# A four-layer decoder in one kernel: a scaled and shifted norm moved into the linear attention's pipeline, with four smaller rearrangements

## The reference

```python
def _L1_attn_ref(x, Wq, bq, Wk, bk, Wv, bv, Wc, We, Wo, bo, gamma, beta):
    residual = x
    ...
    num = einsum('bhsf,bhsfd->bhsd', qf, kv_cum)
    den = einsum('bhsf,bhsf->bhs', qf, cumsum(kf, axis=2))[..., None] + EPS
    o = num / den ...
    y = residual + (o @ Wo + bo)
    return (y - mean(y)) / sqrt(var(y) + LN_EPS) * gamma + beta
# caller: x = x + _L1_attn_ref(_layernorm(x), ...)
# _L1_xattn_ref: "focus" attention on the first 16 tokens of each sequence of x and of ctx
# _L2_attn_ref: Mamba forward and backward; per state s of 16:
#   h = dA_t * h + dBx_t;  y += h * C_t;   dBx = dt * x * B_t
#   then gelu(fwd + bwd + h), a norm, an FFN with gelu
```

## Time and profile before

| | |
|---|---|
| Median of 3 runs | 7387.59 us (7383.5 to 7392.11) |
| The profiled execution | 7383.77 us, span 7382.0 us |
| Busy in the span | PE 6509.4 (88%), DVE 5385.0 (73%), ACT 4114.1 (56%), POOL 2863.0 (39%) |
| Granted TensorE clock, mean | 0.955 of full speed |
| DMA | 190.34 MB, mean 26 GB/s |

### The profile page before, as it was taken

How to read it: one execution, slowest core, us unless ns; L and a number is a source line. 1 busy time by engine, 2 the same in 40 slices (tenths; PEclk the granted TensorE clock), 3 DMA queues, 4 the chain that set the end, 5 groups by cost and what they waited for, 6 DMA issues and landing times. The chain is left out here.

```text
span 7382.0 us, 189639 instructions
## 1 busy us (share of the span) xinstructions
PE 6509.4 (88%) x74836; PEld 3954.8 (54%) x74836; DVE 5385.0 (73%) x8866; ACT 4114.1 (56%) x6062; POOL 2863.0 (39%) x1653
## 2 busy tenths in 40 slices
PE   7989994887697898888998969989899999989998
PEld 5767672443442333333333346667576766667676
DVE  7867476665556999999999955678577777768544
ACT  3556343665446777777766765556344444456433
POOL 3311184332215888888877701156022222211000
PEclk9999997999898999999999989989999999999999
DMA  1000001000001222222212100000000000000000
GB/s 28 0 21 12 2 0 19 3 3 2 15 1 55 74 74 74 74 80 73 73 69 72 58 11 15 10 31 3 12 2 2 2 2 2 2 15 14 2 0 23
DMA packets 115919, 190.34 MB, mean 26 GB/s; under 512 B 38661, under 2 KB 74747, under 8 KB 114971
## 3 DMA queue, kind: packets, MB, share of 16 engines
q1 hardware_dynamic: 115482, 184.01, 7.8%
HBM read 173.87 MB, written 7.98 MB: 25 GB/s over the span
## 5 line engine op out<-in xcount | busy, mean ns | idle before, releaser
L2589 POOL TENSOR_TENSOR m_dBx<-m_dtx,m_Bs 128x1024 f32<-128x1024 f32 x515 | 1205.4, 2357 | 227.6 <-DVE m_hs L2955 185.9
L2955 DVE TENSOR_TENSOR_SCAN m_hs<-m_ps_dA,m_dBx 128x512 f32<-128x512 f32 x1030 | 1199.7, 1204 | 72.5 <-POOL m_dBx L2589 58.2
L2707 PE MATMUL m_ps_y<-m_yc,ident 128*128 128x512 f32 x2060 | 1054.7, 636 | 0.0
L2811 ACT ACTIVATE m_ps_dA<-m_dt,m_A 128x504 f32<-128x504 f32 x1030 | 683.2, 678 | 486.7 <-DVE m_hs L2955 483.9
L2086 POOL TENSOR_TENSOR a_s<-a_s,a_den 128x1024 f32<-128x1024 f32 x128 | 243.7, 1904 | 1125.1 <-DVE a_den L2132 1125.1
L2966 DVE TENSOR_TENSOR m_yc<-m_hs,m_ps_C 128x1024 f32<-128x1024 f32 x515 | 615.0, 1194 | 6.3 <-PE m_ps_C L2688 5.4
L2707 PEld LDWEIGHTS m_ps_y<-m_yc,ident 128*128 128x128 f32 x2060 | 358.7, 194 | 370.4 <-issue 370.4
L2688 PE MATMUL m_ps_C<-m_parts,m_sel 48*128 48x512 bf16 x516 | 203.2, 394 | 204.6 <-DVE m_yc L2966 204.6
L2688 PEld LDWEIGHTS m_ps_C<-m_parts,m_sel 48*128 48x128 bf16 x516 | 47.8, 93 | 606.8 <-DVE m_yc L2966 449.8
L620 POOL TENSOR_TENSOR c_kbd<-c_kf,c_hmask 128x1024 f32<-128x1024 f32 x66 | 125.1, 1895 | 514.3 <-ACT c_kf L530 490.2
L2130 DVE TENSOR_REDUCE a_den<-a_s 128x16 f32<-128x1024 f32 x128 | 156.0, 1219 | 207.9 <-ACT a_s L2038 207.9
(11 more groups left out here) (748 smaller groups left out, 16036.6 us busy)
## 6 DMA issues: line engine op xcount, KB each, us to landing
m_Bs<-BC_rows SPq DMA_DIRECT2D x258, 512.0 KB, 3.5
c_kvb<-in_ctxT SPq DMA_DIRECT2D x68, 128.0 KB, 2.0
c_kvb<-in_ctxT SPq DMA_DIRECT2D x17, 256.0 KB, 2.7
out_dram<-X SPq DMA_DIRECT2D x1, 4096.0 KB
BC_rows<-m_low SPq DMA_DIRECT2D x33, 64.0 KB, 2.8
part_rows<-m_split SPq DMA_DIRECT2D x33, 48.0 KB, 1.7
m_parts<-part_rows SPq DMA_DIRECT2D x33, 48.0 KB, 1.7
m_piece<-BC_rows SPq DMA_DIRECT2D x33, 32.0 KB, 1.7
```

The costliest lines, as they stand in the source:

```text
L2589: return nc.gpsimd.tensor_tensor(to, one, other, ALU.mult)
L2707: last = nc.tensor.matmul(ps_y[:, m, :], C.ident[:], of[:, m, :], start=s == 0, stop=s == NS - 1)
L2811: nc.scalar.activation(seqs(ps_dA[:, h % 3, :]), seqs(dt[:, par, m, :]), ACT.Exp, scale=A[:, second, m, s:s + 1]).then_inc(decay, 1)
L2955: nc.vector.tensor_tensor_scan(hs[:, s % HS, m, :], ps_dA[:, (2 * s + m) % 3, :], dBx[:, s % BX, m, :], 0.0, ALU.mult, ALU.add).then_inc(s ...
```

## The change

(1) `affine_norm` is removed and done inside `attn16_linear`: POOL adds beta to X in `base_rows`; ACT takes var^-0.5 as Ln, drain, Exp per unit (`inverse_root`); DVE has `add_rows` (four `scalar_tensor_tensor` of 128x128 with a drain between the second and third) after `normalise` and ahead of `residual`, and `new_sums` at the slot's end. Three more half units of work follow at the tail. gamma and beta are loaded ahead, and the focus block's weights now load during the linear attention. (2) Focus entry: the context rows are loaded ahead with the weights; x's rows are split between the SP and ACT queues; statistics of the context come first. At its end the DMAs of `C.MV` go by ACT's queue. (3) Mamba's `split_rows`: one cast and three subtractions with two drains, for three casts and two subtractions with four. (4) Table loads: the square root's is issued at the end of many blocks, that of a block's own function right after the root (or by the join ahead of its loop). (5) Mamba's `dBx` multiply runs over the same elements in another order: the innermost run is now the two halves of a state's row.

```diff
@@ act (both scale classes)
-    def act(self, act):
+    def act(self, act, then=None):
...
+        if then is not None:
+            self.C.nc.scalar.preload_act_table(then)
@@ attn16_linear
+            nc.scalar.preload_act_table_set("natural_log_exp_and_others")
...
+            def inverse_root(w, par):
+
+                act.wait_ge(var_ready, w + 1)
+                to = rs2[:, par, :]
+                nc.scalar.activation(to, mv[:, par * UT:(par + 1) * UT, 1], ACT.Ln, bias=eps[:, 0:1])
+                act.drain()
+                nc.scalar.activation(to, to, ACT.Exp, scale=-0.5).then_inc(rs_ready, 1)
+
+            def slot(w, u, weigh=True, root=True):
+                if root:
+                    inverse_root(w - 3, 1 - u)
                 features(w + 2)
...
                 pool.wait_ge(xn_ready, w + 1)
                 pool.sem_inc(begun, 1)
+                x = C.X[:, bass.ds(w * UT, UT), :]
+                nc.gpsimd.tensor_tensor(x, x, bc(beta[:].unsqueeze(1), [P, UT, D]), ALU.add)
...
+            def add_rows(w, u):
+
+                dve.wait_ge(rs_ready, w + 1)
+                for t in range(UT):
+                    y = row(C.Y, w * UT + t)
+                    nc.vector.scalar_tensor_tensor(y, y, mv[:, u * UT + t, 0:1], gamma[:], ALU.subtract, ALU.mult)
+                dve.drain()
+                for t in range(UT):
+                    x = row(C.X, w * UT + t)
+                    nc.vector.scalar_tensor_tensor(x, row(C.Y, w * UT + t), rs2[:, u, t:t + 1], x, ALU.mult, ALU.add)
+
+            def new_sums(w, i, u):
+
+                for t in range(UT):
+                    nc.vector.bn_stats(st2[:, t, :], row(C.X, w * UT + t))
+                dve.drain()
+                for t in range(UT):
+                    nc.vector.bn_aggr(mv2[:, u * UT + t, :], st2[:, t, :])
...
                 mask(w, u)
                 if weigh:
                     normalise(w - 1)
+                if finish:
+                    add_rows(w - 3, 1 - u)
                 if project:
                     residual(w - 2)
                 diagonal_values(w, u)
                 if project:
-                    row_sums(w - 2, i - 1, u)
+                    row_sums(w - 2, u)
+                if finish:
+                    new_sums(w - 3, i - 1 - (1 - u), 1 - u)
@@ mamba, state
-                multiply(dBx[:, s % BX, :, :], dtx[:],
-                         bc(Bs[:, slot, s % CHUNK, :].unsqueeze(1), both)).then_inc(dBx_ready, 1)
+                halves = lambda t: t.rearrange("p m t -> p t m")
+                multiply(halves(dBx[:, s % BX, :, :]), halves(dtx[:]),
+                         bc(Bs[:, slot, s % CHUNK, :].unsqueeze(2), [P, GT, NHF])).then_inc(dBx_ready, 1)
@@ mamba, split_rows
                 nc.vector.tensor_copy(split[:, 0, :], piece[:])
                 dve.drain()
+                nc.vector.tensor_tensor(split[:, 1, :], piece[:], split[:, 0, :], ALU.subtract)
                 nc.vector.tensor_tensor(rest[:], piece[:], split[:, 0, :], ALU.subtract)
                 dve.drain()
-                nc.vector.tensor_copy(split[:, 1, :], rest[:])
-                dve.drain()
-                nc.vector.tensor_tensor(rest[:], rest[:], split[:, 1, :], ALU.subtract)
-                dve.drain()
-                nc.vector.tensor_copy(split[:, 2, :], rest[:]).then_inc(split_ready, 1)
+                nc.vector.tensor_tensor(split[:, 2, :], rest[:], split[:, 1, :], ALU.subtract).then_inc(split_ready, 1)
@@ mamba_join
         def _(act):
+            nc.scalar.preload_act_table(ACT.Gelu)
             with act.Fori(0, steps // 2) as i:
@@ focus_block, sync (then the mirror of it, with r = 2, 3, at the head of the ACT program)
-            for r in range(4):
+            for r in range(2):
                 for b in range(2):
                     at = (2 * r + b) * FT
-                    sp.dma_start(xr[at:at + FT, :, :], C.X[S * b:S * b + FT, r:C.NT:4, :]).then_inc(rows_in[0], 16)
-            by_tile = ctx_rows.rearrange("(m q) t d -> q t m d", q=8)
-            for q in range(8):
-                sp.dma_start(raw_b[q * FT:(q + 1) * FT, :, :], by_tile[q, 0:FT, :, :]).then_inc(rows_in[1], 16)
+                    sp.dma_start(xr[at:at + FT, :, :], C.X[S * b:S * b + FT, r:C.NT:4, :]).then_inc(rows_in, 16)
...
                     sp.dma_start(C.X[S * b:S * b + FT, r:C.NT:4, :], xr[at:at + FT, :, :]).then_inc(returned, 16)
-                    sp.dma_start(C.MV[S * b:S * b + FT, r:C.NT:4, :], mv[at:at + FT, 0, :, :]).then_inc(returned, 16)
```

184 lines of the change are left out of this document (87 added, 97 removed).

## The result

The changed kernel takes 7304.81 us in the median of 4 runs (7294.51 to 7307.8), the kernel before 7387.68; the ratio is 0.9879, with an interval of 0.9866 to 0.9893. That is 83 us less by the medians (89 by the ratio), where 97 were forecast, and inside the range.

What follows compares the result with a forecast made beforehand. DVE was taken to pace the Mamba groups and the linear attention. Terms −2.9 − 11.8 − 18.6 − 34.6 − 28.8 = −96.7 us against the profiled 7383.77 gave 7287, 7291 for the median; range 7255 to 7430.

Steps and rivals of the forecast that it cites:

- Norm in the linear attention: Linear attention and norm stage: removing the separate stage gives −61.8, added DVE work 39.4 + 4.5 + 15; −2.9 us.
- what is unknown is how DVE and POOL disturb each other: Linear attention, `add_rows`: POOL may slow its operations, by 0 to 2.3 us per unit; 0.5 taken, 15 us in all.
- the upper bound of 67 us: Linear attention, `add_rows`: held for one POOL operation's length, 2.3 us, in each unit; as a rival 7343, chance 0.15.
- Focus block: Focus block's entry and exit: earlier context statistics give −7 us, DMAs shared with ACT's queue −4.8; −11.8 in all.
- the last transfer then lands 4.8 us earlier by the rate at which they move: Focus block's exit: with eight DMAs on ACT, SP is done after 7 us and the last transfer lands earlier; −4.8 us.
- Table loads and join: Block starts, two attentions and the join: ACT's table loads leave the path; −7.2, −2.4 and −9, together −18.6 us.
- 1.03 us for each of seven block starts: Block starts: DVE's 1.35 us wait for ACT's root loses 1.03 when the table is there; seven counted, −7.2 us.
- Split of the C rows: Mamba's split: last casts no longer held up by POOL's addition, −23, and a shorter split, −11.6; −34.6 us.
- the 11.6 us of the shorter split: Mamba's split: an operation and two drains fewer save some 0.35 us in each of 33 cases; −11.6 us.
- Order of dBx: Mamba's `dBx` multiply on POOL: about 2.1 us for 2357 ns, 0.9 gained per group over 32 groups; −28.8 us.
- five dBx stand in the chain that ends in the 1.28 us wait, so 0.26 less on each ends it: Mamba group: faster multiplies on POOL remove DVE's wait for `dBx`; of this 0.9 us per group is taken as gained.
- The slow `dBx`: Mamba's multiply on POOL: striding makes it slower, at 3.1 us +131 and 7451, at 3.33 us 7566; chance 0.20.
- The order changes nothing: Mamba's `dBx` multiply stays at 2.36 us, so the 28.8 us are not gained and the kernel takes 7320; chance 0.15.

Runs made afterwards that it cites:

- the merge: Kernel before with only the norm moved into the linear attention, the separate norm stage removed: 7356.97 us in one run, beside 7386.21.
- the filled kernel: Changed kernel with four unused 128x128 f32 PE matmuls added per unit of the linear attention, ahead of the scores: 7280.64 us, ratio 0.9854.
- the second profile of the same kernel: Changed kernel run again without an edit, on another chip than at first: 7305.41 us, ratio 0.9886.
- the pairs: Changed kernel with dtx and dBx stored with the two halves of a state side by side in memory: 7284.77 us, ratio to before 0.9847.

## Why the prediction was right, and where it wasn't

The direction and the range held, and the sum came within 14 us. The stages' sums came out near for reasons that in part cancel, which is luck, and one effect larger than most of the terms, the Mamba block's gain from the merge, was in no term. Point by point:

**Norm in the linear attention (forecast −2.9, measured +0.9; +4.2 in its stage alone, with 28.9 us less in the Mamba block).** DVE's share was sized well: 1.36 us per unit forecast, 7.74 − 6.51 = 1.23 measured at full clock. The step that failed is "what is unknown is how DVE and POOL disturb each other", taken at 15 us. `add_rows` met POOL only at times, and then beside an operation of 0.73 us, not 2.3: its first two operations sum to 23.3 us over the block, in the filled kernel 20.3. With the filling matmuls, so without the long units, the linear attention is 278.5 − 236.5 = 42.0 us longer than before, and DVE's share alone was put at 39.4 + 4.5 = 43.9: next to nothing is left for contention. The Trainium skill ("SBUF — State Buffer", "Who interferes with whom") has a DVE instruction with two SBUF inputs and a GpSimd instruction that reads SBUF contend, and the one issued later blocked until the earlier one ends. The row at 1024.16 agrees: two operations take 1.09 us beside POOL's 0.78, for 0.61 alone; the upper bound of 67 us was far off because the POOL operations that stand there are short. What did cost 22 us was nowhere in the sum: the wait for PE was taken as a resource to be filled (0.69 us per unit), and filling it on DVE made PE the engine that idles, whose clock then fell to its lower level, 1.2 GHz, in about one unit of four. The wrong 15 us for contention stood in for it, and so the stage came out nearly as forecast, by luck.

**Focus block (−11.8; −12.9 in the profile, 10 by its two ends).** That the profile shows −12.9 is luck: the block's middle was short in it, and in the second profile of the same kernel the block takes 800.8 us, 1.1 less than before. The entry gave 8.8 for 7: besides the statistics, DVE no longer waits for x's rows at all; it starts on them 10.0 us after the first issue, for 11.5. Whether the second queue or the missing transfers of the context's rows bring them earlier wasn't tried apart. The exit gave 1.1 for 4.8. The failed step is "the last transfer then lands 4.8 us earlier by the rate at which they move": the same megabyte of `C.X` still crosses, and moving the DMAs of `C.MV` to ACT's queue freed SP's issue time, which was not the bound.

**Table loads and join (−18.6; −13.1 in the profile, −10.6 by the means of the profiles).** In the join DVE's wait for ACT fell by 8.8 us, as forecast (5.4 for the first piece stays), but its idle time without a releaser rose from 1.1 to 2.7, so 7.2 of 9 came. Outside it the failed step is to count 1.03 us for each of seven block starts. DVE's wait for the root fell by up to 1.02 us at them, from 1.34 to 0.33 at most, yet only the LoRA and the top-k FFN got shorter, by 2.0 and 1.4 us in the mean: at the other starts something else sets the time. What that is wasn't followed.

**Split of the C rows (−34.6; alone −34.2).** Right in size, wrong in half its reason. All held casts vanished, as taken. But the 11.6 us of the shorter split were not gained. Held casts alone don't come to 34 us either: in the profile of the merge alone, which has no stops, the 11 held casts lengthen their groups by 18.5 us in all. A good part of the rest lies in the seven groups with a stop, which take 18 us less in the split's profile than in that of before, 5 of them for three held casts.

**Order of dBx (−28.8; alone nothing measurable, about −14 in plain groups).** The price taken, 2.1 us, was 2.28. And the step "five dBx stand in the chain that ends in the 1.28 us wait, so 0.26 less on each ends it" failed at its anchor: the chain doesn't start from DVE, it starts when ACT's `m_ln` comes, and its end sets when DVE goes on. From POOL's first addition to the scan that waits it is 25.08 us before, 24.63 in the changed kernel and 23.91 with the pairs, in groups of 58.51, 58.05 and 57.35: the rest is 33.4 us each time. So a plain group is as long as the stretch up to `m_ln` and POOL's ten operations: what shortens them counts in full (0.41 for the order), what shortens DVE ahead of the wait counts nothing (the split). The split's and the order's parts of the wait, +0.35 and −0.42, cancel, which is why it stands at 1.25 after all. Together the forecast for Mamba was off by 1.2 us through errors that cancel, which is luck: 11.6 us too much for the shorter split and 14.5 for the order (0.46 by 31 groups is 14.3, for 28.8), against the stops, which the forecast didn't know and which go with the merge, by 28.9 us between the two profiles. The last 35.7 us, from the merge alone to the changed kernel, are the held casts and the shorter plain groups.

**The rivals.** The slow `dBx` fell by measurement. Its price had a slip besides: 49.09 + 16 × 0.74 is 60.9 us of POOL work per group, not 61.5, so 7432 and not 7451. "The order changes nothing" was nearer the truth than the forecast for the order alone on the kernel before, whose time it didn't change, though the operation did get faster.

## What to carry to other kernels

When work is moved onto the engine that paces a loop, look at what the others then do with the time: where PE idles more, its clock may fall for whole iterations, and a few cheap matmuls that nobody needs can be worth more than they cost. Where one engine waits for another in every iteration, savings ahead of that wait on the waiting engine only lengthen the wait (here 1.28 to 1.6 us); follow the releaser's chain back to where it starts, and shorten that. A block that is removed can change the time of one that starts 1000 us later and isn't edited: compare every stage, not only the edited ones. Where a sum comes out right, check its terms by parts made alone: here several were off by 10 us and more and cancelled. And before a block's 2 us are put down to an edit, see how much that block moves without it.
